# Building a graph's adjacency matrix with windows of 5 destinations instead of 10, and a ring of one-hot rows made partly by ScalarE

## What is computed

```python
deg  = segment_sum(ones(E + N), dst_with_loops)
norm = dinv[src] * dinv[dst]                 # dinv = deg ** -0.5
h = leaky(batchnorm(x @ W1 + b1)); h = h / norm_of(h)
for _ in range(5):
    m = h @ W
    agg = segment_sum(m[src] * norm[:, None], dst) + bias
    h = leaky(batchnorm(agg))
```

## Time and profile before

| | us |
|---|---|
| median of 3 runs (5368.89 to 5371.68) | 5371.18 |
| span of the profiled execution | 5371.2 |
| busy in that span: PE | 3946.3 |
| DVE | 3302.9 |
| POOL | 3612.1 |
| ACT | 1686.0 |

### The profile page before, as it was taken

The page is one execution under the profiler, slowest core; times in us unless marked ns, Lnnn a source line. Parts: engine busy times, 40 slices in busy tenths (PEclk is TensorE's granted clock), DMA queues, the critical chain, the costliest instruction groups (busy, mean ns, idle before and its releaser), DMA issues. The chain is left out here.

```text
span 5371.2 us, 95369 instructions
## 1 busy us (share of the span) xinstructions
PE 3946.3 (73%) x25259; PEld 2539.3 (47%) x25260; DVE 3302.9 (61%) x9981; ACT 1686.0 (31%) x4268; POOL 3612.1 (67%) x4256
## 2 busy tenths in 40 slices
PE   4446666666649999999999677776777776667775
PEld 2212222222224544545454356666666666666664
DVE  5999999999930211202020377777777777777777
ACT  0046666666620000101010143333333333333332
POOL 1057777788777777777710057777777777777773
PEclk9989999999979999999999788899998899989888
DMA  6613232323379999998978344444444444444442
GB/s 257 241 43 126 91 135 91 137 88 111 119 202 334 310 323 320 312 329 299 339 257 291 120 124 128 128 129 128 129 128 128 129 129 129 128 128 128 129 129 80
DMA packets 319595, 940.56 MB, mean 175 GB/s; under 512 B 76889, under 2 KB 144333, under 8 KB 317608
## 3 DMA queue, kind: packets, MB, share of 16 engines
q1 hardware_dynamic: 173648, 615.36, 33.9%
q0 software_dynamic: 145824, 323.92, 21.3%
HBM read 735.23 MB, written 203.77 MB: 175 GB/s over the span
## 5 line engine op out<-in xcount | busy, mean ns | idle before, releaser
L741 POOL DMA_INDIRECT records<-recs,poss x1562 | 1621.8, 1038 | 492.8 <-issue 492.8
L1375 POOL DMA_INDIRECT kv<-kv_table,rec x1664 | 1608.0, 966 | 443.7 <-issue 429.1
L901 PE MATMUL ps<-adj,mh 128*128 128x500 f16 (+1 forms) x6370 | 1315.4, 366 | 0.0
L1413 PE MATMUL ps<-msg,ohf 128*128 128x136 f32 x3328 | 554.0, 315 | 620.3 <-DVE msg L1473 618.6
L573 PE MATMUL ps<-h 128*128 128x490 f16 x2500 | 653.4, 386 | 399.0 <-ACT h L674 367.8
L901 PEld LDWEIGHTS ps<-adj,mh 128*128 128x128 f16 x6370 | 619.8, 97 | 686.3 <-issue 35.6
L1413 PEld LDWEIGHTS ps<-msg,ohf 128*128 128x128 f32 x3328 | 462.6, 209 | 696.1 <-DVE msg L1473 349.5
L528 DVE TENSOR_SCALAR h<-iota,rel 128x490 f16<-128x490 f16 x2500 | 771.1, 369 | 0.0
L1055 DVE SCALAR_TENSOR_TENSOR h<-ps,vecs,deg (+1 forms) x65 | 46.7, 718 | 1122.5 <-PE ps L901 1122.5
L1464 DVE TENSOR_TENSOR kq<-kv,ps 128x512 f32<-128x512 f32 x416 | 285.6, 687 | 561.7 <-DMA kv<-kv_table,rec 544.8
L573 PEld LDWEIGHTS ps<-h 128*128 128x128 f16 x2500 | 201.5, 100 | 850.9 <-ACT h L674 557.0
(11 more groups left out here) (265 smaller groups left out, 4475.8 us busy)
## 6 DMA issues: line engine op xcount, KB each, us to landing
adj<-adj_full SPq DMA_DIRECT2D x420, 875.0 KB, 5.8
adj_full<-blk SPq DMA_DIRECT2D x12, 6125.0 KB, 18.8
records<-deg SPq DMA_DIRECT2D x1, 59840.0 KB, 174.1
rec<-records SPq DMA_DIRECT2D x416, 136.0 KB
recs<-in_edge_attr POOLq DMA_DIRECT2D x142, 352.0 KB, 5.9
kv<-kv_table,rec POOLq DMA_INDIRECT x1664
records<-recs,poss POOLq DMA_INDIRECT x1563
adj<-adj_tail SPq DMA_DIRECT2D x35, 437.5 KB, 3.8
```

Source lines behind the costliest of these rows:

```text
L741: G.indirect_dma_start(out=k.rec_d, out_offset=bass.IndirectOffsetOnAxis(ap=k.poss[:, q, j:j + 1], axis=0), in_=k.recs[:, q, j, :], in_off ...
L901: last = mm(bank, mh[:, part, hi, :], adj[:, c, x * width:(x + 1) * width], start=False, stop=True, skip_group_check=True)
L1375: G.indirect_dma_start(out=kv[:, q, j, :], out_offset=None, in_=k.kv_d, in_offset=bass.IndirectOffsetOnAxis(ap=rec[:, q, j, RD:RD + 1].bit ...
L1413: last = mm(PS[:, 6 + q % S, 0:MW], ohf[:, q, j, :], msg[:, q, j, :], start=(j == 0), stop=(j == GT - 1))
```

## The change

Windows become 5 destinations (WD = 5, WC = 245), so there are 1250, in groups of 10 and blocks of 100 (the same 500 destinations); a window takes three tiles.

- The lo one-hots no longer belong to a window. They go into a ring of 64 tiles, each made once: DVE makes 8 or 9 of each group's 12.5 with a compare against a scalar (`spread`), ACT makes four, a group ahead, by distance and Relu. PE addresses the ring by the tile's number.
- The column one-hots of a window's three tiles are made by one two-input compare, [128 x 245 x 3]: constant columns `codes` (eight tables, one for each window mod 8) against three 16-bit codes `k.code16`. PE reads them with a step of three elements.
- Two windows share a PSUM bank, and ACT evacuates both at once. PSUM holds eight windows.
- Degree sums go from ACT into a small buffer and from there to DRAM by SP, block by block; `convolve` begins with their load.
- In `prepare` the first and last tile come from running minima and maxima (two scans) and counts with an accumulator, ten on DVE and ten on ACT. 16-bit codes and the fast path's conditions are made too.
- In the adjacency block's head POOL makes the eight tables. SPLIT stays at 17.

```diff
-WD = 10
+WD = 5
-WCODE = 512
-BW = 50
+WCODE = 256
+PH = 8
+BW = 100
-WPP = 5
-FAST = 4
-TW = 16
+WPP = 10
+FAST = 3
+TW = 32
+RING = 64
+AHEAD_LO = 18
+TWO = 25
...
+                L(V.tensor_scalar(df[:, 0:T], wf[:, 0:T], 1.0 / PH, -(PH - 1) / (2.0 * PH), ALU.mult, ALU.add))
+                L(V.tensor_scalar(df[:, 0:T], df[:, 0:T], RNE, RNE, ALU.add, ALU.subtract))
+                L(V.scalar_tensor_tensor(hf[:, 0:T], wf[:, 0:T], float(WC - WCODE), k.code[:, :], ALU.mult, ALU.add))
+                L(V.scalar_tensor_tensor(k.code16[:, 0:T], df[:, 0:T], float(-WC * PH), hf[:, 0:T], ALU.mult, ALU.add))
...
-                V.tensor_copy(k.loh[:, :], k.lo[:, :])
...
+                V.tensor_tensor_scan(least[0:WP, ::-1], tmn[0:WP, ::-1], tmn[0:WP, ::-1], float(N), ALU.min, ALU.min).then_inc(sem("least_ready"), 1)
+                L(V.tensor_tensor_scan(most[0:WP, :], tmx[0:WP, :], tmx[0:WP, :], 0.0, ALU.max, ALU.max))
...
                 for j in range(WPP):
-                    V.scalar_tensor_tensor(m[0:WP, 0:T], tmn[0:WP, 0:T], w4[0:WP, 0, j:j + 1], up[0:WP, 0:T], ALU.is_lt, ALU.mult)
-                    L(V.scalar_tensor_tensor(n[0:WP, 0:T], tmx[0:WP, 0:T], thr[0:WP, j:j + 1], down[0:WP, 0:T], ALU.is_ge, ALU.mult))
-                    V.tensor_reduce(w4[0:WP, 1, j:j + 1], m[0:WP, 0:T], AX.X, ALU.max)
-                    L(V.tensor_reduce(w4[0:WP, 2, j:j + 1], n[0:WP, 0:T], AX.X, ALU.max))
...
+                    V.tensor_scalar(eq[0:WP, j % 2, 0:T], most[0:WP, 0:T], thr[0:WP, j:j + 1], None, ALU.is_lt, ALU.add,
+                                    accum_out=w4[0:WP, 1, j:j + 1]).then_inc(starts, 1)
...
+            @block.scalar
+            def _(act):
...
+                    nc.scalar.activation(eq[0:WP, 2 + j % 2, 0:T], least[0:WP, 1:T + 1], ACT.Sign, bias=over[0:WP, j:j + 1],
+                                         accum_out=w4[0:WP, 2, j:j + 1]).then_inc(sem("ends_counted"), 1)
...
+        def tiles_of(g):
+            return AHEAD_LO + g * TWO // 2
+        def of_act(g):
+            a = tiles_of(g) + tiles_of(g) % 2
+            return a, a + 2
...
+                for f in range(PH):
+                    nc.gpsimd.iota(codes[:, f, :, :], [[1, WC], [0, FAST]], base=f * WC, channel_multiplier=0,
+                                   allow_small_or_imprecise_dtypes=True)
...
+                def spread(t):
+                    V.tensor_scalar(ohl[:, bass.ds(t & (RING - 1), 1), :].rearrange("p a c -> p (a c)"), iota[:, 0:P],
+                                    k.lo[:, bass.ds(t, 1)], None, ALU.is_equal)
...
                         for x in range(WPP):
                             v.wait_ge(done, w + x + 1)
-                            lo_onehots(ohl[:, q, 0:JV[x], :], first[x], JV[x])
-                            if x == 0:
-                                v.wait_ge(rel_ready, gr + 2)
-                            for j in range(FAST):
-                                last = V.tensor_scalar(ohc[:, q, j, :], iota[:, :], rel[:, par, x, j:j + 1], None, ALU.is_equal)
-                            last.then_inc(ready, 1)
+                            V.tensor_tensor(ohc[:, (w0 + x) % SL, :, :], codes[:, (w0 + x) % PH, :, :],
+                                            k.code16[:, bass.ds(first[x], FAST)].rearrange("p (o j) -> p o j", o=1).broadcast_to([P, WC, FAST]),
+                                            ALU.is_equal).then_inc(ready, 1)
...
+                for t in range(AHEAD_LO):
+                    spread(t)
...
+                        for t in spread_of(h):
+                            spread(v.snap(i * (2 * TWO) + t))
...
                 def group(gr, w0):
+                    first = firsts_of(PE, gr)
+                    long = entry(nc, PE, k.wt, gr * TW + 3 * WPP, 0, 1)
+                    pe.wait_ge(ready_lo, gr * 2 + 2)
...
+                            if q % 2 == 0:
+                                pe.wait_ge(put, gr * (WPP // 2) + x // 2 + 1)
                             pe.wait_ge(ready, w + 1)
-                            pe.wait_ge(ready_lo, w + 3)
                             for j in range(FAST):
-                                last = nc.tensor.matmul(PS[:, q, 0:WC], ohl[:, q, j, :], ohc[:, q, j, :],
-                                                        start=(j == 0), stop=(j == FAST - 1))
+                                last = nc.tensor.matmul(banks[:, q * 256:q * 256 + WC],
+                                                        ohl[:, bass.ds((first[x] + j) & (RING - 1), 1), :].rearrange("p a c -> p (a c)"),
+                                                        ohc[:, (w0 + x) % SL, :, j], start=(j == 0), stop=(j == FAST - 1))
...
+                def put_pair(r, q, y, slot):
+                    act.wait_ge(done, r * 2 + SL + 2)
+                    A.activation(blk[:, q, :].rearrange("p (h x d) -> p h x d", h=NB, d=WD)[:, :, 2 * y:2 * y + 2, :],
+                                 banks[:, slot * 512:(slot + 1) * 512].rearrange("p (x c) -> p x c", x=2)[:, :, 0:WC].rearrange("p x (h d) -> p h x d", d=WD),
+                                 ACT.Copy, scale=0.25).then_inc(put, 1)
...
+                def distances(t, n):
+                    for j in range(2):
+                        last = A.activation(away[:, n, j, :], iota[:, 0:P], ACT.Abs, bias=k.lo[:, bass.ds(t + j, 1)], scale=-1.0)
+                    last.then_inc(away_ready, 1)
+                def onehots(t, n, nth):
+                    act.wait_ge(away_ready, nth + 1)
+                    A.activation(ohl[:, bass.ds(t & (RING - 2), 2), :], away[:, n, :, :], ACT.Relu, bias=1.0, scale=-1.0).then_inc(ready_lo, 1)
...
+                def degree(b, q, width):
+                    sp.wait_ge(deg_free, b + 2)
+                    sp.dma_start(k.deg_d[bass.ds(b * BD, width)].rearrange("(o c) -> o c", o=1), degs[0:1, q, 0:width]).then_inc(deg_moved[q], 16)
...
-                sp.dma_start(k.deg_d.rearrange("(p c) -> p c", p=1), k.deg[0:1, :]).then_inc(deg_moved, 16)
-                sp.wait_ge(deg_moved, 16)
```

More of the change, by code:

```diff
@@ L161, in prepare @@
         hf, df, wf = (k.deg[:, TPL * REC + x * TC:TPL * REC + (x + 1) * TC] for x in range(3))
-        tmn, tmx, up, down = (k.h[:, x * TC:(x + 1) * TC] for x in range(4))
+        tmn, tmx, most, least = (k.h[:, x * TC:(x + 1) * TC] for x in range(4))
         hih = sb("hih", [P, TC], FP16)
-        thr = sb("thr", [P, WPP], FP32)
+        thr, over = sb("thr", [P, WPP], FP32), sb("over", [P, WPP], FP32)
         w4 = sb("w4", [P, 8, WPP], FP32)
+        home = sb("home", [P, 1], FP32)
         tab = sb("tab", [P, TW], I32)
@@ new lines, in _ @@
+                v.wait_ge(starts, WPP)
+                L(V.tensor_tensor(tmx[0:WP, 0:T - 1], most[0:WP, 2:T + 1], least[0:WP, 0:T - 1], ALU.subtract))
+                L(V.tensor_reduce(small[0:WP, 4:5], tmx[0:WP, 0:T - 1], AX.X, ALU.max))
+                L(V.tensor_scalar(w4[0:WP, 3, :], w4[0:WP, 1, :], float(T - FAST), None, ALU.min))
+                L(V.tensor_scalar(home[0:WP, :], home[0:WP, :], 0.5, None, ALU.mult))
+                L(V.tensor_scalar(w4[0:WP, 0, :], w4[0:WP, 3, :], home[0:WP, 0:1], None, ALU.subtract))
@@ L491, in _ @@
             def _(g):
-                nc.gpsimd.iota(iota[:, :], [[1, WC]], base=0, channel_multiplier=0, allow_small_or_imprecise_dtypes=True)
+                nc.gpsimd.iota(iota[:, :], [[1, 256]], base=0, channel_multiplier=0, allow_small_or_imprecise_dtypes=True)
                 nc.gpsimd.memset(k.gate[:], 0.0)
@@ new lines, in onehots, with block_of @@
+                def onehots(t, n, nth):
+                    act.wait_ge(away_ready, nth + 1)
+                    A.activation(ohl[:, bass.ds(t & (RING - 2), 2), :], away[:, n, :, :], ACT.Relu, bias=1.0, scale=-1.0).then_inc(ready_lo, 1)
+                def block_of(q, b, pairs, i):
+                    more = 2 * TWO // 2 * (GB // 2)
+                    start = 0 if type(b) is int and b == NBLK else q
+                    of = (lambda t: act.snap(i * (2 * more) + t)) if i is not None and type(b) is not int else \
+                         (lambda t: (NBLK // 2 * 2 * more if start != q or b == NBLK else 0) + t)
+                    for y in range(pairs):
+                        g, x = divmod(y, WPP // 2)
+                        nth = (b * GB + g + 1) * 2
+                        begins = of_act(q * GB + g + 1)
+                        exists = type(b) is not int or b * GB + g + 1 < WP
+                        if exists and x in (0, 2):
+                            act.wait_ge(done, (b * GB + g) * WPP + SL)
+                            distances(of(begins[x // 2]), x // 2)
+                        if y == 0:
+                            if i is not None:
+                                act.wait_ge(stored[q], 16 * i)
+                            act.wait_ge(summed, b + 1)
+                        put_pair(b * (BW // 2) + y, q, y, (q * (BW // 2) + y) % 4)
+                        if exists and x in (0, 2):
```

(15 more changed lines are left out.)

219 lines of the change are left out of this document (101 added, 118 removed).

## The result

The changed kernel takes 5957.8 us (5952.6 to 5960.3), the kernel before 5370.1 us beside it: ratio 1.109, 95% interval [1.108, 1.111]. The forecast of 5290 us was wrong by 668 us and in sign. Lines in rows of the changed kernel are those of its own source: L630 is the window matmul, L574 the 735-element compare, L564 the one-hot of `spread`, L693 ACT's evacuation, L808 POOL's scatter, L537 the table reads.

A forecast was written before the change was run, and what follows sets the result against it. The prediction took POOL's share of the scatters, last at the adjacency barrier, as the bound. From 5371.2 us, -85 (POOL's share) + 6.0 (POOL's head) - 0.5 (preparation) + 0.3 (table) - 2.0 (convolution head) gave 5290 us, range 5256 to 5352.

The forecast's parts named there:

- PE's matmul: Adjacency: each 245-column window matmul bounded by 0.11 and 0.22 us, taken as 0.12; PE's group then 6.0 us.
- Rival C: Adjacency: PE or the hand-offs set the pace; at 10 us a group the kernel takes 5431 us; chance 0.08.
- DVE's group: Adjacency: ten compares at 0.54 us and 8.5 one-hots at 0.2 make 7.1 us a group.
- Rival B: Adjacency: the 735-element compare runs one element a cycle, 10.0 us a group, kernel 5431 us; chance 0.07.
- POOL's rate: Adjacency: DVE slows POOL's indirect DMAs less, so POOL's share takes 1119 us instead of 1203.5: -85 us.
- Rival A: Adjacency: new two-input compares hold POOL back as L528 did, 0.148 us a scatter; kernel 5347 us; chance 0.10.
- POOL's head: Start of adjacency: eight 735-column iotas at 0.75 us each and a larger base table, hidden by nothing: +6.0 us.
- The tail: End of adjacency: 11 us from DVE's last compare to PE's end, all done near 1215 us, before POOL.
- ACT never late: Adjacency: ACT needs 5.3 us a group, works a group ahead and stays faster than DVE.
- the preparation: Stage before adjacency: five rounds and a cast dropped, scans and counts added: -0.5 us (-8.5 to +3).
- the convolution's head: Start of convolution: degrees already stored block by block, so SP no longer sends them first: -2.0 us.
- rival D: Adjacency: windows don't fit three tiles or the ring, so the slow branch runs; some 1550 us more; chance 0.02.

The follow-up runs named there:

- a_static: The changed kernel with PE's window-matmul weights read from a fixed buffer of zeros instead of the ring: 5674.7 us.
- v3: v2 with three one-input compares for each two-input one, eight slots between DVE and PE, and contiguous moving operand: 5350.8 us, ratio 0.9966 to the kernel before.
- v2_nolong: v2 without the slow branch for wide windows on DVE and PE: 7074.7 us, on a chip where the kernel before took 6827.
- v1: The changed kernel with a 50-slot ring, one register operation a matmul, one table read a group, codes made by DVE: 6459.6 us, ratio 1.011 to the kernel before.
- b_split16: The kernel before with added bounds and SPLIT = 16, one scatter round moved from adjacency to convolution: 5422.2 us, ratio 1.008.
- v2: v1 with PE's row of the table on a 64-byte boundary; run only in variants, so no time of its own.
- two flat runs: The changed kernel with PE reading 245 contiguous columns instead of every third, alone and with fixed weights: 6005.5 and 5689.3 us.

## Why the prediction was wrong, point by point

- **PE's matmul** is the step that failed. "I bound it by 0.11 and 0.22, twice as long" was a guess with no row behind it, and the row that existed, 0.39 us of busy time for a matmul, tells nothing of a sequencer. The sum took 0.12 for each matmul and 6.0 us for PE's group. Measured, 30 x 0.318 = 9.5 us, with 5.1 degree matmuls at 0.415 instead of 0.24 (the clock had fallen to 0.56 of full while PE waited on its sequencer), a table read of 1.4 us and PE's waits for DVE give the 13.9 us a group of (2076.5 - 341.2) / 125. Rival C was the case; it had 0.08 and its price, 10 us a group, was too low by 3.9. Fixed weights took back 285 of the 588 us; the rest is DVE's group.
- **DVE's group**, 7.1 us, measured 11.6 (a_static) by the same sum: the compare 0.58, not 0.54 (0.4 a group); `spread` 0.305, not 0.2, set by three register operations (0.9); the table reads, counted on PE and forgotten on DVE, 1.9; the jump, 4.7 us in four groups, 1.2. Rival B, a compare at one element a cycle, was not the case. The two elements a cycle that the Trainium skill allows such a compare ("Vector Engine (DVE) Microarchitecture Reference", 5.1 Performance modes) fit the measured 0.58 us; the estimate worked out from them, 0.54, was 0.04 short.
- **POOL's rate** was worth -85 + 6. In the changed kernel its share took 1178.5 us (333.4 to 1511.9) instead of 1203.5, only 25 less, though DVE's compares were much rarer than forecast. The step that failed is the reading of rows 4: 0.97 beside L508 and 1.34 beside L528. From two single instructions I made L528 the culprit, and overlooked the line of DVE just before them:

```profile
903.96 0.54 DVE L508 TENSOR_TENSOR h<-iota,loh 128x384 f16<-128x384 f16 x1
```

  An L508 was running when the scatter of 904.00 began; beside the one of 900.07 it began half a microsecond later. All scatters in 400:1400 of the kernel before say the same: the 117 that began at most 0.2 us after an L508 took 1337 ns on average, the 53 that had L528 but no L508 beside them (over 0.8 of their first 0.96 us) 993. So L508, the two-input compare, is what held POOL there. The runs agree: one-input compares at 66% of the time left the scatter at 1017 ns (v3), two-input ones at 66% made it 2330 (v2_nolong: 1140 in 1000 us, 0.58 each). Rival A was right as a mechanism and mis-sized: it had 0.148 us a scatter, and 2330 against 971 ns is 1.36. In the changed kernel it stayed small (1068 ns), where PE held DVE back to 711 compares in 1000 us; with 935 it was 1298 (v1). The rule of the Trainium skill ("SBUF — State Buffer", Who interferes with whom), that a DVE instruction with two SBUF inputs contends with POOL, agrees with these runs; I had set a row against it. I had also said that the trace agrees with a lock-out by DVE's two-port modes; the one-input compares of these runs, 1017 ns beside them in v3, show none.
- **POOL's head**, +6.0: the iotas took 29.7 us instead of 5.7, since I scaled by columns and not by the length of the inner run. The first record load began at 333.44 instead of 306.47.
- **The tail**: the 11 us "that today lie between DVE's last compare (1469.2) and PE's end" left out SP's last block store, 17 us more, which POOL had covered: in the kernel before it landed at 1503.17, 22 us after ACT's end.
- Right: that POOL was last in the kernel before, though b_split16 could not bear it out; ACT never late (4.7 us busy a group against the 5.3 forecast, 0.582 an evacuation); the preparation (barrier at 299.5 instead of 302.6, of which 2.4 us were an earlier start: -0.7 against -0.5); the convolution's head (stage 1519.6 instead of 1522.3, -2.7 against -2.0); no wide window (3750 = 3 x 1250 matmuls, rival D).

Open: the hand-offs of over 1 us on three of the chips; what makes DVE's sequencer pause at a jump back; what made v2's DVE faster than v1's; the 48 and 15 us of the two flat runs; whether the moved round would have gained anything in the kernel before without the added bounds.

## What to carry to other kernels

Count a sequencer's instructions as you count an engine's: here each register operation ahead of an instruction cost 0.07 us on DVE and 0.09 on PE, and an engine whose instruction is shorter than their sum runs at the sequencer's pace. A ring whose length makes the slots repeat with the unrolled loop needs none on the engines that fill it. Look at what a sequencer does after a loop's jump back, and look again after each edit, even one in a branch that never runs. Before an engine next to POOL gets a two-input operation, price what POOL loses; a faster instruction there can be the slower kernel. And what the last engine covers (a store, a read) must be added again once another one is last.

## What the runs showed of the hardware that was not expected

- PE: a weight load with three register operations ahead of it came every 0.318 us, with one every 0.134. DVE: a 128-column one-hot with three came every 0.305 us, with one every 0.163.
- Two-input fp16 compares of DVE, 0.58 us each and nearly back to back, made POOL's indirect DMAs 2330 ns; 1298 with 935 of them in 1000 us, 1068 with 711; 973 with 472 compares of 147 elements, 971 with DVE quiet, 988 and 1017 beside one-input compares at 39% and 66% of the time.
- A DVE loop that executes 282 instructions lost 4.7 us at each jump back, one with 368 2.8, one with 208 only 0.27. One with 198 lost 0.24, and 3.3 to 3.5 when a branch that it jumps over grew.
- A table read of eleven values on PE took 2.69 us from an offset of 40 bytes and 1.32 on a multiple of 64; ten took 1.08.
- A POOL iota of 735 fp16 values took 3.7 us in runs of three and 0.71 in one run.
- Matmuls of 245 columns with fixed weights came 0.164 us apart at the fast pace with a step of three fp16 values in the moving operand, 0.109 with contiguous ones.
